# Staggering the two sequences through the first layers, and softmax sums split between TensorE and VectorE, in an eight-layer sequence model

## The reference, cut to what matters

```python
x = x + _L0_attn_ref(_layernorm(x), ...)   # cosformer attention, projection, RMS norm, GELU feed-forward
x = x + _L0_ffn_ref(_layernorm(x), ...)    # channel mix
x = x + _L1_attn_ref(_layernorm(x), ...)   # causal softmax attention, 16 heads, keys and values from 32 latents
x = x + _L1_ffn_ref(_layernorm(x), ...)    # mixture of 32 experts, sorted by expert

# _L0_attn_ref after its attention sum:
h = x + output @ out_w + out_b
m = rmsnorm(h, norm2_w)
return h + jax.nn.gelu(m @ mlp_w1 + mlp_b1) @ mlp_w2 + mlp_b2

# _L0_ffn_ref:
xr = mu_r * x + (1.0 - mu_r) * x_prev
xk = mu_k * x + (1.0 - mu_k) * x_prev
k_act = jnp.square(jax.nn.relu(xk @ W_k.T))
out = jax.nn.sigmoid(xr @ W_r.T) * (k_act @ W_v.T)

# _L1_attn_ref:
attn = jax.nn.softmax(jnp.where(mask, q @ k.T / sqrt(64), neg_inf), axis=-1)
y = attn @ v
```

## Time and profile before

| | before |
|---|---|
| median of 3 runs | 5653.43 us (5645.69 to 5659.54) |
| the profiled execution's own time | 5696.46 us |
| its span, first to last instruction | 5694.9 us |
| TensorE busy | 4378.5 us, 77% |
| VectorE busy | 3661.7 us, 64% |
| GpSimd busy | 2281.8 us, 40% |
| ScalarE busy | 1786.3 us, 31% |
| mean granted TensorE clock | 0.858 of full |

### The profile page before, as it was taken

The page is one execution under the profiler, slowest core; times in us unless marked ns, Lnnn a source line. Parts: engine busy times, 40 slices in busy tenths (PEclk is TensorE's granted clock), DMA queues, the critical chain, the costliest instruction groups (busy, mean ns, idle before and its releaser), DMA issues. The chain is left out here.

```text
span 5694.9 us, 86289 instructions
## 1 busy us (share of the span) xinstructions
PE 4378.5 (77%) x31912; PEld 2428.5 (43%) x31912; DVE 3661.7 (64%) x10829; ACT 1786.3 (31%) x2787; POOL 2281.8 (40%) x2766
## 2 busy tenths in 40 slices
PE   6969797888879796776778778687787886877872
PEld 4444444454535453443343443434443434344341
DVE  4565656565556565458677686685776866768765
ACT  2424242423333323333224232332232422423230
POOL 3333332323333333556336244372362533624435
PEclk9989898989989898887878888888788888888885
DMA  3000000000000001760000000000000000000000
GB/s 122 11 15 16 9 16 9 16 9 16 9 16 10 15 10 57 226 188 14 14 16 7 17 10 9 14 9 17 14 6 18 9 10 17 9 17 11 9 14 4
DMA packets 143893, 147.30 MB, mean 26 GB/s; under 512 B 31180, under 2 KB 128142, under 8 KB 142926
## 3 DMA queue, kind: packets, MB, share of 16 engines
q1 hardware_dynamic: 116286, 94.67, 5.6%
q0 software_dynamic: 18432, 37.79, 2.3%
q10 hardware_dynamic: 8736, 8.91, 0.5%
HBM read 70.83 MB, written 63.11 MB: 24 GB/s over the span
## 5 line engine op out<-in xcount | busy, mean ns | idle before, releaser
L919 DVE CUSTOM_DVE_ANT_0 twin<-twin,w_mask_row 128x512 f32<-128x512 f32 (+3 forms) x2048 | 950.9, 520 | 333.1 <-PE twin L1891 331.4
L1891 PE MATMUL twin<-arena 32*128 32x128 f32 (+3 forms) x4096 | 809.4, 522 | 37.0 <-DVE arena L919 16.9
L1909 PE MATMUL twin<-arena 32*128 32x128 f32 (+3 forms) x4096 | 795.9, 507 | 31.1 <-DVE arena L919 29.7
L1554 ACT ACTIVATE arena<-twin 128x768 f32<-128x768 f32 (+1 forms) x544 | 478.9, 880 | 674.4 <-PE twin L1920 387.9
L1909 PEld LDWEIGHTS twin<-arena 32*128 32x128 f32 x4096 | 351.9, 202 | 482.0 <-issue 293.6
L827 POOL TENSOR_SCALAR ve<-mv 128x4 f32<-128x4 f32 x128 | 27.5, 215 | 1158.2 <-DVE mv L879 1157.5
L377 POOL DMA_INDIRECT got<-sorted_y,back x288 | 278.1, 966 | 495.7 <-ACT ring L1758 306.2
L1836 PE MATMUL twin<-w_ident_b 128*128 128x512 bf16 x1200 | 344.5, 438 | 132.3 <-DVE mv L879 50.3
L1891 PEld LDWEIGHTS twin<-arena 32*128 32x128 f32 x4096 | 361.0, 208 | 196.2 <-issue 109.0
L369 POOL DMA_INDIRECT sorted_x<-got,w_mo_first_slots x288 | 284.1, 986 | 139.7 <-issue 65.5
L1932 PE MATMUL twin<-arena 128*32 128x128 f32 (+3 forms) x2944 | 304.1, 457 | 9.0 <-POOL arena L712 9.0
(11 more groups left out here) (440 smaller groups left out, 9392.6 us busy)
## 6 DMA issues: line engine op xcount, KB each, us to landing
sorted_y<-arena SPq DMA_DIRECT2D x96, 256.0 KB, 2.8
sorted_x<-zeros ACTq DMA_DIRECT2D x2, 4096.0 KB, 20.0
a<-sorted_x SPq DMA_DIRECT2D x64, 128.0 KB, 2.5
b<-sorted_x SPq DMA_DIRECT2D x64, 128.0 KB, 3.0
hres<-sorted_x SPq DMA_DIRECT2D x64, 128.0 KB, 2.5
x<-x_in SPq DMA_DIRECT2D x18, 256.0 KB, 3.4
sorted_x<-got,w_mo_first_slots POOLq DMA_INDIRECT x288
x_next<-kept_x SPq DMA_DIRECT2D x18, 256.0 KB, 2.8
```

The source lines that it names most:

```text
L919: last = dve.tensor_tensor_reduce(s[:, e, at:at + w], s[:, e, at:at + w], W["mask_row"][:, T - w:T], -1.0, 3e38, ALU.add, ALU.min, into)
L1554: act.activation(at_pt[tag][n % len(at_pt[tag])][:, :, 0:w], twin[SLOT["scores_t", c, u] % 3][:, :, 0:w], ACT.Exp, scale=1.0 if tag == "l1 ...
L1891: last = pe.matmul(s[:, e, at:at + w], queries[r, P * i:P * (i + 1)], keys[r, 0:w], start=(at == 0), stop=True, skip_group_check=True)
L1909: last = pe.matmul(s[:, e, at:at + w], keys[r, P * m:P * (m + 1)], queries[r, P * m:T], start=(at == 0), stop=(tag == "l2"), skip_group_ch ...
```

## The change

It does four things, all in the first loop.

1. In the stretch between the attention sum of layer 0 and `l1_attention`, every engine's list is rewritten: q = 0 goes one step ahead of q = 1. The projection of q = 0 moves into the attention loop of layer 0 (after quartet `c4` = 6), and the two projections write to other banks (`l0_out`). Of the seven `keep_busy` groups of this stretch and the entry of `l1_attention`, five go.
2. In `l0_attention`, the two scans of a sequence are done in two different quartets, and `take_state` comes between the two `weigh_lags` of a quartet.
3. Four of GpSimd's 16 row sets are sent after the reciprocal roots of the RMS norm instead of ahead of them, two behind each.
4. In `l1_attention`, `sums` is replaced. TensorE still sums the first 128 columns of key tile 0 (`first_sums`, step 5). The other columns, 128 to 511, of all key tiles are first added together on VectorE into `at_sum` (part of `ring`): `merge_first` (two of 2 x 384 columns, steps 4 and 5), `merge_second` (two of 2 x 256, steps 0 and 1 of the next turn of the loop), `merge_third` (two of 2 x 128, step 1). Then TensorE sums the merged tile once (`merged_sums`, step 2). `invert` and `turn_max` move a step back, `divide` from step 2 to step 3, `values(c - 1, 2)` a step ahead. ScalarE's exponentials wait for the merges that read the tile they overwrite.

```diff
+                            def merge_first(c, h):
+                                dve.wait_ge(sg["l1_masked"], STEPS_OF * c + 3 + h)
+                                if c >= 2:
+                                    dve.wait_ge(sg["l1_sums"], c - 1)
+                                dve.tensor_tensor(at_sum[c % 2][:, h], at_pt["l1"][h][:, :, P:T], at_pt["l1"][2 + h][:, :, 0:T - P],
+                                                  ALU.add).then_inc(sg["l1_merged"], 1)
+                            def merge_second(c, h):
+                                into = at_sum[c % 2][:, h, :, P:T - P]
+                                dve.wait_ge(sg["l1_masked"], STEPS_OF * c + 5 + h)
+                                dve.wait_ge(sg["l1_merged"], STEPS_OF * c + 2)
+                                dve.tensor_tensor(into, into, at_pt["l1"][4 + h][:, :, 0:2 * P], ALU.add
+                                                  ).then_inc(sg["l1_merged"], 1)
+                            def merge_third(c, h):
+                                into = at_sum[c % 2][:, h, :, 2 * P:T - P]
+                                dve.wait_ge(sg["l1_merged"], STEPS_OF * c + 3 + h)
+                                dve.tensor_tensor(into, into, at_pt["l1"][4 + h][:, :, 2 * P:3 * P], ALU.add
+                                                  ).then_inc(sg["l1_merged"], 1)
                             for c in range(-2, QUARTETS + 1):
                                 for u in range(STEPS_OF):
                                     maxima(c + 2, u)
                                     beside(c, u)
-                                    if u == (2 if tag == "l1" else 5):
+                                    elif u < 2:
+                                        merge_second(c - 1, u)
+                                        if u == 1:
+                                            merge_third(c - 1, 0)
+                                            merge_third(c - 1, 1)
+                                    elif u == 3:
                                         divide(c - 1)
+                                    elif u >= 4:
+                                        merge_first(c, u - 4)
...
+                            biased(0)
+                            take_attention(0)
+                            biased(1)
+                            divide(1)
+                            rms_apply(0, HR[0], B[0], "l0_b2")
+                            take_attention(1)
+                            add_attention(0)
+                            rms_apply(1, HR[1], B[1], "l0_b2")
+                            add_attention(1)
...
+                            take_mlp(0)
+                            layernorm_apply(0, "c_a")
+                            mix(0)
+                            take_mlp(1)
+                            square(0)
+                            layernorm_apply(1, "c_a")
+                            take_mix(0)
+                            mix(1)
+                            layernorm_apply(0, "l1_a")
+                            square(1)
+                            take_mix(1)
...
+                            def merged_sums(c):
+                                pe.wait_ge(sg["l1_merged"], STEPS_OF * (c + 1))
+                                for j in range(HG):
+                                    last = pe.matmul(bank[7][rows_of(j), P:T], W["ones"][:, 0:LAT],
+                                                     at_sum[c % 2][:, 1 - j // 2, j % 2], start=False, stop=True,
+                                                     skip_group_check=True)
+                                last.then_inc(sg["l1_sums"], 1)
...
                                         if u == 0:
                                             values(c - 1, 1)
                                         elif u == 1:
-                                            sums(c - 1, 2)
+                                            values(c - 1, 2)
                                         elif u == 2:
+                                            merged_sums(c - 1)
+                                        elif u == 3:
                                             turn_max(c + 1)
-                                            values(c - 1, 2)
-                                        elif u == 3:
-                                            sums(c, 0)
                                         elif u == 4:
                                             values(c, 0)
                                         else:
-                                            sums(c, 1)
+                                            first_sums(c)
...
+                                if c4 == HG + 2:
+                                    project(0)
+                            keep_busy(pb(0, 0), (None, 0))
+                            project(1)
...
+                            turn(0, B[0], "l0_b2", 1, "l0_turn3")
+                            up(0)
+                            turn(1, B[1], "l0_b2", 2, "l0_turn3")
+                            down(0)
+                            up(1)
+                            turn(0, A[0], "c_a", 1, "c_turn")
+                            down(1)
+                            keys_gates(0)
+                            mixed_values(0)
+                            turn(1, A[1], "c_a", 2, "c_turn")
+                            keys_gates(1)
+                            mixed_values(1)
```

138 lines of the change are left out of this document (76 added, 62 removed).

## The result

The changed kernel takes 5551.02 us (median of four, 5545.44 to 5558.58) where the kernel before takes 5651.65 us: ratio 0.9824, 95% interval 0.9804 to 0.9843, 100.6 us less. I had forecast 5655 us, no change.

The account below looks back on a forecast made before the run. TensorE was taken to bound the pair loop, hand-overs with no engine saturated the stretch before it. Terms -7.0 + 0 + 4.0 + 2.5 + 0.7 = +0.2 us a turn, eight turns +1.6: 5655 us, range 5585 to 5712.

Parts of the forecast that it names:

- mask collisions: Pair loop: VectorE's additions and GpSimd's masks wait for each other; 0 to +6 us a turn, +2.5 taken.
- clock in the loop: Pair loop: TensorE's clock may fall below 1.00 with 2.3 us idle in 14.2; +0.7 us a turn.
- +1.15 us each: Pair loop: five quartets lengthen to 14.2 us, 1.15 more than now; +5.7 us a turn.
- the -0.6 of an early one: First quartet (c = 0): VectorE has room and TensorE gets faster; -0.6 us a turn.
- the -2.8 of the drain: Two draining quartets: VectorE has room and TensorE gets faster; -2.8 us a turn.
- The clock term: Stretch: half-clock spell after TensorE's idle piece, 1.2 us lost from the reordering's 8.2 us gain, leaving -7.0.
- It can't be packed: Pair loop: VectorE's 12.65 us of work a quartet leaves gaps, since `merged_sums` makes TensorE wait for the last addition.
- from there VectorE has no gap: ... 10.1 us: Pair loop: after step 4's scores, VectorE's maxima, additions and 0.5 us of hand-overs take 10.1 us; quartet 14.2.
- half of the collisions hold up GpSimd instead: Pair loop: reason for taking +2.5 us a turn for collisions, below the middle of 0 to +6.
- my rival of +6 us: Pair loop: every collision with a mask counts, +6 us a turn instead of +2.5; 5683 us, chance 0.10.
- the rival of 5703 us: Pair loop: TensorE's clock oscillates, +6 us a turn, +48 us in all; chance 0.20.
- the rival of short hand-overs: Pair loop: additions and masks miss each other, no clock falls; -20 to -50 us, about 5620; chance 0.20.

Follow-up runs that it names:

- b_again: The kernel before, unedited, profiled again on the third group's chip: 5647.51 us (one run).
- a_again: The changed kernel, unedited, beside the kernel before on the second group's chip: 5637.86 us, ratio 0.9904.
- a_third_on_pe: Changed kernel with a quartet's two 256-column additions taken from VectorE; TensorE adds that block by four matmuls in `merged_sums`: 5589.21 us, ratio 0.9833 to the kernel before.
- a_third_fill: Changed kernel with the two 256-column additions done by TensorE and a filler group before the second sequence's keys: 5522.20 us, ratio 0.9768 to the kernel before.
- a_extra_addition: Changed kernel with one more VectorE addition of 768 columns in each quartet: 5662.48 us, ratio 0.9951 to the kernel before.
- b_more_fillers: Kernel before with two more groups of six filler matmuls a turn in the stretch's idle pieces: 5627.55 us, ratio 0.9960.
- the first two groups: First and second of four groups of experiments, each on its own chip; the kernel before took 5694.86 and 5690.62 us there.
- the other two: Third and fourth groups of experiments, each on its own chip; the kernel before took 5646.47 and 5649.95 us there.

## Why the prediction was wrong

Two chips without late signals, `b_again` against the changed kernel, means over the eight turns' windows, in us:

| part of a turn | predicted | before | after | measured |
|---|---|---|---|---|
| `l0_attention` | 0 | 44.2 | 44.7 | +0.5 |
| stretch to the first scores | -7.0 | 51.7 | 41.8 | -9.9 |
| first scores to last quartet | +4.0 | 86.3 | 83.7 | -2.6 |
| last quartet, drain | -1.7 | 38.5 | 37.4 | -1.1 |
| tail | +1.7 | 4.6 | 6.2 | +1.6 |
| mask collisions | +2.5 | | | in the rows above |
| clock in the loop | +0.7 | | | 0, in the rows above |
| sum | +0.2 | | | -11.5, eight turns -92 |

Of the five middle quartets at +1.15 us each, four stand in the third row, with the -0.6 of an early one, and the fifth in the fourth, with the -2.8 of the drain. The two spans differ by 93.3 us (5645.9 and 5552.6), so nothing of weight lies outside this table.

**The stretch.** The reordered lists were right: at full clock 48.5 against 40.8 us, -7.7, where I had -8.2. The clock term had the wrong sign. I charged the new order 1.2 us for a spell behind its long idle piece; that spell is there (6.8 us at half clock, 41.8 against 40.8, so 1.0). What I left out is what the old order pays: 51.7 against 48.5, 3.2 us. That makes +1.0 - 3.2 = -2.2 us where I had +1.2. The step that failed is to take the kernel before's clock from the one profile shown (0.97, one spell of 3.4 us) as a property of the kernel. Turns of one execution differ: in the fourth of `b_again` spells of 3.4 and 13.7 us cost 4.6 us more than two of 3.4 us in the fifth, though TensorE's idle pieces ahead of them are the same, none over 2.0 us.

**`l0_attention`.** Right. The 7.4 us between the two profiles that were there to compare are late signals where before's was taken, shown by `a_again` and `b_again`: either kernel takes 44 to 45 us without them and 52 with them. The sign was in the recorded text and I passed over it: the profiled execution stood 0.8% above the median, about what chips differ by.

**The pair loop.** "It can't be packed" was right in its mechanism: TensorE waits for the last addition, and from it to the maxima of step 4 it takes 3.95 us (4.05 predicted). The step that failed is "from there VectorE has no gap: ... 10.1 us". It takes 12.93 - 3.95 = 8.98. I added up durations, and their starts lie closer: a 512-column addition shown as 0.69 is followed after 0.60 (965.00 to 965.60), one of 768 shown as 0.95 after 0.87 (973.95 to 974.82), a maxima step of 1.37 takes 1.23 (970.31 to 971.54), because the accumulator's read of 0.14 lies under the next instruction (both at 971.54). Over the ten pieces the overlaps make 0.9 us, and of the 0.5 us of hand-overs only 0.22 is seen. So a quartet comes to 12.9, a little under the 13.06 of before, instead of 14.2. `a_third_on_pe` and `a_third_fill` confirm VectorE's chain as the bound: 0.67 us less of it and 0.2 to 0.3 more of TensorE give 12.93 to 12.48. TensorE's own bound is near by then: it is busy for 12.30 of the 12.48 us.

The early quartets, in which VectorE has room, gained 2.0 us (11.33, 9.78, 11.66 to 11.33, 8.84, 10.63), not 0.6: I had counted one, and two gained about 1 us each. In the first of these two no sums stand yet; of the change it has only the later place of `turn_max`, and no run tries that alone. The drain behind the last quartet gained 0.9 and not 2.8. The tail's +1.7 came out as +1.6 for another reason (the clock) than the three additions that I had named.

**Collisions with masks.** The collisions are there, and who waits goes by who came first. Where VectorE's addition had started, GpSimd's mask or copy waited for it, and the addition kept its price; in the middle quartets all but short overlaps of masks and copies with additions are of this kind, and the VectorE chain loses nothing. So there "half of the collisions hold up GpSimd instead" should have read all of them. GpSimd's masks went from 405 to 535 and from 632 to 683 ns in the mean, and its first copy of a group of row maxima from 252 to 708. In the drain it is not so. Where a mask had started first, the addition waited (1.37 us for 0.95), and GpSimd is on the chain: the last mask of a turn starts at 1033.80, 0.33 us after its exponential has ended (1032.66 and 0.81), because the send ahead of it lasts 1.50 us in place of 0.97; VectorE waits 0.75 us for that mask. That is one reason why the drain gained less than I had; how much all collisions cost there was not tested. Nothing reaches my rival of +6 us. The rule of the Trainium skill (SBUF — State Buffer, "Who interferes with whom"), that the pair is an exclusive lock, agrees with the masks that wait. I drew from it that the upper end would hold; what I left out is the order of the two, by which in these rows it is mostly GpSimd that waits.

**The clock in the loop.** 1.00 in all middle quartets, against the rival of 5703 us. TensorE's wait is 0.86 us in 12.9, not 2.3 in 14.2. That the mechanism exists is shown by `a_extra_addition`, whose fourth quartet has a clock of 0.79 and costs 2.4 us more than its neighbours.

**A sum that does not come out.** For the rival of short hand-overs I had "-7.0 + 3.0 to -1 a turn" and wrote -20 to -50 us. Read as -7.0 and something from 3.0 to -1, the terms give -4 to -8 a turn, -32 to -64 us; the 5620 us of this rival is then its slow end. The measured -101 us lies below either.

## What to carry to other kernels

Price a gapless run of one engine by the distance from start to start of its instructions in the trace, not by adding their durations: here the difference of 10% decided whether the quartets came out longer or shorter. Before a wait of TensorE is moved, look at the granted clock of the same stretch in several turns of the loop, since what the old order loses to it may differ from turn to turn, and a few filler matmuls show what it is worth (3.2 us a turn here). Compare two profiles only after the unchanged kernel has been profiled on the second one's chip.

## What the runs showed of the hardware

- Signals of TensorE can come 0.6 to 3.4 us, single ones later still, after the recorded end of their matmul, in `l0_attention` and the later layers, for every kernel on the chips of the first two groups, and (but for three signals, of 4.5 us) for none on those of the other two: 7 to 8 us a turn in `l0_attention`. In all that is 44 us for the kernel before (5691 and 5647) but 87 for the changed one (5638 and 5551): the old stretch is shorter where signals come late (49.8 and 51.7 us), while the new one and its quartets lose a little (42.6 and 41.8, 13.2 and 12.93). So the same change is worth 1.0% on one chip and 1.8% on another. The cause was not found; that the late stretches of `l0_attention` lie where groups of four sends are under way was seen in one profile only.
- With a GpSimd instruction and a VectorE addition of two SBUF operands at once, the one that started second waited: masks of 256 columns grew from 0.41 to 0.87 us behind additions of 512 columns and to 1.09 behind those of 768, and an addition of 768 grew from 0.95 to 1.37 us behind a mask of 512. Overlaps of 0.2 us or less, and sends that had started first, did not lengthen an addition of 512 or 768 columns by more than 0.04 us.
- VectorE's additions follow each other closer than they last: one recorded as 0.69 us after 0.60, one of 0.95 after 0.87.
- TensorE's clock fell to half behind idle pieces of at most 2.0 us in the stretch of `b_again`, in every turn, and stayed full there once fillers stood in them (`b_more_fillers`); it stayed full over waits of 0.86 us in each quartet of the changed kernel.
- The same instructions of the stretch took 50.0 us in one turn and 54.7 in the next.
